# A two-layer graph network on one core: layer 1's turn with both halves of Y and their sums put first, and layer 0's gathers awaited by groups of 8 tiles

## The reference

```python
# layer 0: an edge network, summed over the edges of a destination
h = leaky_relu(concat(x[dst], x[src] - x[dst]) @ W1 + b1, 0.01)
h = leaky_relu(h @ W2 + b2, 0.01)
x = layernorm(x + segment_sum(h, dst))
# layer 1: attention with 4 heads, self loops added to the edges
xw = (x @ W).reshape(N, 4, 64)
logits = leaky_relu(a_src[src] + a_dst[dst], 0.2)
ex = exp(logits - segment_max(logits, dst)[dst])
alpha = ex / segment_sum(ex, dst)[dst]
x = layernorm(x + segment_sum(xw[src] * alpha, dst).mean(heads) + bias)
```

## Time and profile before

| | |
|---|---|
| median of three executions | 9346.02 us |
| profiled execution | 9348.76 us |
| its span (first to last instruction) | 9346.8 us |
| TensorE matmul busy | 6164.8 us, 66% |
| TensorE weight loads | 4718.3 us, 50% |
| VectorE | 5858.3 us, 63% |
| ScalarE | 3903.2 us, 42% |
| GpSimd | 6102.1 us, 65% |
| granted TensorE clock, mean | 0.863 |
| DMA | 301.41 MB, 32 GB/s |

### The profile page before, as it was taken

One profiled execution on the slowest core, in us unless ns is written; L12 is line 12 of the kernel. 1 busy time (PEld: TensorE's weight loads), 2 busy tenths in 40 slices (PEclk: granted clock), 3 DMA queues, 4 the chain that ended last, 5 costly groups with the idle time before them and its releaser, 6 DMA issues.

```text
span 9346.8 us, 206356 instructions
## 1 busy us (share of the span) xinstructions
PE 6164.8 (66%) x47166; PEld 4718.3 (50%) x47167; DVE 5858.3 (63%) x14312; ACT 3903.2 (42%) x10077; POOL 6102.1 (65%) x6281
## 2 busy tenths in 40 slices
PE   3477777777777767775366666666666666666675
PEld 2355555555555555553244444444444444444454
DVE  4355555555555555554477777777777777777753
ACT  1244444454444444442144444444444444444431
POOL 0777777777777777770577767676776767667600
PEclk6788888888888888996689989899998998989875
DMA  2211111111111111110311111111111111111100
GB/s 62 46 40 40 40 40 40 39 40 39 40 40 40 40 40 40 40 39 2 37 30 29 28 27 28 27 28 27 28 27 27 28 27 28 27 26 28 25 0 14
DMA packets 301370, 301.41 MB, mean 32 GB/s; under 512 B 194201, under 2 KB 197606, under 8 KB 301064
## 3 DMA queue, kind: packets, MB, share of 16 engines
q0 software_dynamic: 200704, 265.33, 15.2%
q1 hardware_dynamic: 98580, 32.69, 2.0%
q10 hardware_dynamic: 2068, 3.20, 0.1%
HBM read 286.10 MB, written 16.30 MB: 32 GB/s over the span
## 4 chain that ended last, share of the span: by engine, by line
DVE 23%; POOL 23%; issue 22%; PE 18%; DVEq 5%; ACT 3%; ACTq 2%; POOLq 1%; DMA 1%; SPq 0%
POOL big L361 23%; DVE S L464 7%; PE ps L905 6%; PE pu L891 4%; DVE state L655 2%; DVE rel L461 1%; DVE rowA L604 1%; POOLq L352 1%; DVE rowD L609 1%; PE ps L788 1%; DVE Y L636 1%; DVEq L671 1%; ACT ST L1063 1%; DVE zz L676 1%; DVE mnew L696 1%
## 5 line engine op out<-in xcount | busy, mean ns | idle before, releaser
L361 POOL DMA_INDIRECT big<-x_dram,idx x3136 | 3085.8, 984 | 1561.3 <-issue 1196.2
L361 POOL DMA_INDIRECT big<-q_dram,idx x3136 | 3015.3, 962 | 1201.8 <-issue 1197.3
L891 PE MATMUL pu<-Y,S 128*128 128x265 f32 x7856 | 2138.6, 417 | 746.2 <-DVE Y L636 738.9
L891 PEld LDWEIGHTS pu<-Y,S 128*128 128x128 f32 x7856 | 1489.9, 200 | 1035.2 <-issue 790.3
L636 DVE TENSOR_TENSOR Y<-big,ps 128x1040 f32<-128x1040 f32 x982 | 1210.1, 1232 | 659.8 <-ACT ps L1067 573.6
L464 DVE TENSOR_TENSOR S<-ps,rel 128x1024 f32 x978 | 1197.7, 1225 | 224.9 <-DVE rel L461 224.5
L981 ACT COPY ST<-ps 128x512 bf16<-128x512 bf16 x978 | 537.3, 586 | 1744.7 <-PE ps L788 1744.7
L802 PE MATMUL pu<-rowX,S 128*128 128x192 bf16 x3936 | 580.6, 264 | 1009.4 <-issue 765.7
L501 DVE TENSOR_TENSOR Y<-Y,rowX 128x512 f32<-128x512 f32 x491 | 340.5, 693 | 1256.9 <-ACT rowX L993 1238.9
L802 PEld LDWEIGHTS pu<-rowX,S 128*128 x3936 | 383.4, 98 | 1207.0 <-issue 1093.0
L905 PE MATMUL ps<-identb,S 128*128 128x128 bf16 x3912 | 550.6, 231 | 519.1 <-DVE S L464 518.5
(11 more groups left out here) (167 smaller groups left out, 8683.2 us busy)
## 6 DMA issues: line engine op xcount, KB each, us to landing
big<-q_dram,idx POOLq DMA_INDIRECT x3136
big<-x_dram,idx POOLq DMA_INDIRECT x3136
rowD<-dst_dram SPq DMA_DIRECT2D x196, 32.0 KB
q_dram<-state SPq DMA_DIRECT2D x3, 1568.0 KB, 20.2
x_dram<-big SPq DMA_DIRECT2D x1, 3381.0 KB, 39.8
idx<-srcT_dram SPq DMA_DIRECT2D x98, 32.0 KB, 1.8
dstc<-dstT_dram SPq DMA_DIRECT2D x98, 32.0 KB
out<-big SPq DMA_DIRECT2D x1, 3104.0 KB
```

Source lines behind the costliest of these rows:

```text
L361: nc.gpsimd.indirect_dma_start(o, None, x_dram if l else q_dram, bass.IndirectOffsetOnAxis(ap=idx[:, half, t:t + 1], axis=0)).then_inc(gat ...
L891: last = t_.matmul(bank, Sf[:, t, :], Y[:, t, :], start=(t == 0), stop=(t == 7))
```

## The change

In layer 1 the halves are no longer kept apart. VectorE does both `weigh` calls at the start of its turn, TensorE both `sums` calls before the transposes, and ScalarE exponentiates the weights `w` first in its turn and does both `ends` for turn n-1 (half 1 had been done a turn later). In layer 0 the gathers of a group raise a semaphore of their slot (16 of them, `slot`); SyncE waits for group after group, raises `ready`, and after eight groups `gdone`. TensorE waits for `ready` before each group and no longer for a chunk. SyncE's own work in layer 0 is written out: it counts a chunk's groups, then loads the lists of the chunk two further on. Core of the diff:

```diff
+        slot = [[sem(f"slot{p}{r}") for r in range(GS)] for p in range(2)]
+        ready = sem("ready")
...
-                 "lz": 1, "dw": 1, "w": 1, "sf0": 1, "sf1": 2, "y0": 2, "y1": 2, "U0": 2, "U1": 2, "nz": 3,
+                 "lz": 1, "dw": 1, "w": 1, "sf0": 1, "sf1": 1, "y0": 2, "y1": 2, "U0": 2, "U1": 2, "nz": 3,
...
+                if arrive is not None:
+                    arrive(g)
+                    apart(eng)
...
+            def landed(q, half):
+
+                apart(sp)
+                for r in range(GS):
+                    sp.wait_ge(slot[half][r], q * (16 * TG) + 16 * TG)
+                    sp.sem_inc(ready, 1)
+                sp.sem_inc(gdone, 1)
+
+            for i in range(2):
+                chunk(0, i, i)
+            with sp.Fori(0, (NS - 2) // 2) as q:
+                for half in range(2):
+                    landed(q, half)
+                    chunk(0, q * 2 + (half + 2), half)
...
-                            ).then_inc(gath[l][half], 16)
+                            ).then_inc(gath[half] if l else slot[half][r], 16)
...
                         weigh(k, 0, at)
+                        weigh(k, 1, at)
...
-                    if k.has(2):
-                        weigh(k, 1, at)
...
-                pe.wait_ge(gath[0][half], q * (16 * TS) + 16 * TS)
-                pe.sem_inc(gdone, 1)
-                steps(pe, 0, i, first0, turn0(half))
+                steps(pe, 0, i, first0, turn0(half), lambda g: pe.wait_ge(ready, g + 1))
...
                     sums(k, 0)
+                    sums(k, 1)
...
-                if k.has(2):
-                    sums(k, 1)
...
-                    if k.has(2):
-                        ends(k, 1, 2)
+                    if k.has(1):
+                        k.after("dw", 1)
+                        k.after("y1", 2)
+                        a_.activation(wb[:, :, :], dw[:, :, :], ACT.Exp).then_inc(m["w"], 1)
...
                     if k.has(1):
-                        ends(k, 0, 1)
+                        ends(k, 0)
...
                     if k.has(1):
-                        k.after("y1", 2)
-                        a_.activation(wb[:, :, :], dw[:, :, :], ACT.Exp).then_inc(m["w"], 1)
+                        ends(k, 1)
```

More of the change, by code:

```diff
@@ L157, in build @@
         dst_in = [sem("dst_in0"), sem("dst_in1")]
-        gath = [[sem(f"gath{l}{p}") for p in range(2)] for l in range(2)]
+        gath = [sem(f"gath{p}") for p in range(2)]
+        slot = [[sem(f"slot{p}{r}") for r in range(GS)] for p in range(2)]
+        ready = sem("ready")
         row_in = sem("row_in")
@@ L241, in apart, with steps @@
             eng.sem_inc(idle, 1)
-        def steps(eng, l, i, first, turn):
+        def steps(eng, l, i, first, turn, arrive=None):
             apart(eng)
@@ L294, in _, with chunk @@
             sp.wait_ge(s["t_out"], 32)
[L296 to L315, removed]
+            def chunk(l, i, half):
+                sp.wait_ge(gdone, i + (l * NS + 1))
+                sp.dma_start(idx[:, half, :], srcT_dram[:, ds(i * TS, TS)]).then_inc(idx_in[half], 16)
+                sp.wait_ge(fredge_flatd, i + (l * NS + 1))
+                sp.dma_start(dstc[:, half, :], dstT_dram[:, ds(i * TS, TS)]).then_inc(dst_in[half], 16)
@@ new lines, in landed @@
+            def landed(q, half):
[10 more added lines that the diff above has]
+                    chunk(0, q * 2 + (half + 2), half)
+            for i in range((NS - 2) // 2 * 2, NS):
+                landed(i // 2, i % 2)
+                if i + 2 < NS:
+                    chunk(0, i + 2, i % 2)
@@ new lines, in _, with chunk1 @@
+            sp.wait_ge(tab1["v"], 2 * (NB // 2) + 1)
+            sp.dma_start(x_dram.rearrange("(b p) d -> p b d", p=P), x1).then_inc(x_out, 16)
+            def chunk1(i, q, half):
+                chunk(1, i, half)
+                sp.wait_ge(sgv, i * 4 + 1)
+                for h in range(H):
+                    sp.dma_start(rowD[h * GS:(h + 1) * GS, :],
+                                 dst_dram[ds(i * (GS * GE), GS * GE)].rearrange("(g e) -> g e", g=GS)
+                                 ).then_inc(row_in, 16)
@@ L317, in _ @@
+            sp.wait_ge(s["d_out"], 32)
+            supers(sp, chunk1)
             sp.wait_ge(L[1]["acc"], STEPS + PAST)
@@ L592, in lk @@
                     dve.wait_ge(dvs, i * 8 + n)
-                dve.wait_ge(gath[1][half], q * (16 * TS) + 16 * TS)
+                dve.wait_ge(gath[half], q * (16 * TS) + 16 * TS)
                 dve.sem_inc(gdone, 1)
@@ L1027, in _, with ends @@
             copied(tab1, D)
-            act_tiles = Past(act, "act_tile", 2, 2 * TS - TG)
+            act_tiles = Past(act, "act_tile", 1, 2 * TS - TG)
             act_blocks = Past(act, "act_block", 3, NB - 1)
-            def ends(k, h, back):
-                k.after(f"U{h}", back + 1)
-                at = act_tiles.back(back - max(k.tail, 0))
+            def ends(k, h):
+                k.after(f"U{h}", 2)
+                at = act_tiles.back(1 - max(k.tail, 0))
                 a_.copy(Y[:, h * 4:h * 4 + 4, UW:YW], edgeE[:, ds(at + h * 4, 4), :])
-                a_.copy(Sf[:, h * 4:h * 4 + 4, :], S[:, ds(((k.sn + back) % 2) * TG + 4 * h, 4), :]
+                a_.copy(Sf[:, h * 4:h * 4 + 4, :], S[:, ds(((k.sn + 1) % 2) * TG + 4 * h, 4), :]
                         ).then_inc(L[1][f"sf{h}"], 1)
@@ L1052, in turn @@
                         a_.copy(Mx[:, ds(b, 1), :], mnew[:, :].unsqueeze(1)).then_inc(m["mb"], 1)
-                    if k.has(3):
                         k.after("e", 3)
```

## The result

The changed kernel takes **9692.75 us** (median of 3, 9691.95 to 9694.01) against 9346.02: ratio 1.0377, 95% interval 1.0363 to 1.0391. It is slower by 347 us, where the forecast was 8938 and the range ended at 9087. The profiled execution has a span of 9692.1 us.

What follows compares the result with a forecast made beforehand. GpSimd paces layer 0; turns of 7.63 us set layer 1's chunk, and GpSimd would after the change. Span 9346.8 less 400 (layer 0's 53 included) and 8 for the last chunk gives 8939; forecast 8938 us, range 8885 to 9087.

Steps and rivals of the forecast that it cites:

- Layer 0: End of layer 0: one turn of about 7 us behind the last landing instead of 60.5, so -53 us.
- The wait for `w`: Layer 1: VectorE's 1.31 us wait per turn for ScalarE's weights, before the first half of Y, goes.
- TensorE alone: Layer 1's turn, transposes to transposes: copy wait, `ad`, two sums; 6.5 us, and up to 0.4 for branch and waits.
- The 14.1 us of maxima and restart: Layer 1: the part of each chunk outside its turns, kept at 14.1 us beside 9.98 turns of 6.7.
- The clock: Rival: TensorE falls to 1.2 GHz in layer 1, turns up to 11.1 us; 9910 with half of them; chance 0.04.
- GpSimd's bound: Layer 1: unhindered gathers at 1.294 us each, 82.8 us a chunk, would set the pace after the change.
- the prediction's first rival: Layer 1's turn stays above 6.87 us and turns set the chunk: 9087 at 7.2 us, 8987 at 7.0; chance 0.25.
- The slower rival: TensorE at 1.2 GHz in layer 1; slower than before once a chunk passes 91.3 us; 9910 with half; chance 0.04.

Runs made afterwards that it cites:

- ad first: The changed kernel with `ad` moved from the end of TensorE's turn to the head of the next in layer 1: 8967.14 us, 8955.08 when repeated.
- the filled one: The kernel with `ad` at the head of the next turn, plus five unread matmuls behind each turn's transposes in layer 1: 8944.71 us, ratio 0.9569.
- fill_both: The changed kernel plus five unread matmuls behind the transposes and eight behind `ad`: first run 13506.34 us beside 13963.45 for the kernel before; repeat 9408.21 us.

## Why the prediction was wrong

- **Layer 0** was right in mechanism and low in size: -53 forecast, -65 to -70 measured alone. Groups are awaited (704.5 us of TensorE's idle time there end with SyncE's L313), one turn is left behind the last landing, and SyncE's counting held nothing up: the gathers of layer 0 wait for their own issue alone (1200.3 us). Why gathers run at 1.260 instead of 1.267 us in layer 0 wasn't tried.
- **The wait for `w`** went, as forecast: no idle time before Y ends with ScalarE in the kernel after. VectorE now waits for TensorE's sums there (550.6 us in the page's group of L660).
- **The step that failed** is the loop "TensorE alone": "6.5 us, and up to 0.4 for the turn's branch and waits, which no row shows apart here". The rows did show it. In the earlier trace rows the sums start at 7008.32, 1.25 us behind the `ad` before them, with VectorE's Y named as the releaser. But Y was done at 7007.59, 0.73 us before that start. What was left had no releaser but TensorE's own sequencer, and the rest of its work had run under half 1's matmuls, `ad` and the wait for Y. Bare, it is 1.76 us in 343 of the 441 turns and 0.51 in the other 98 (means over the gaps between the last `ad` and the first sums). Where it is 0.5, the turn is 6.65 us in the mean, as forecast. The forecast rested on the minority. A turn into a new group takes 7.70 us even where all of its sums run at full clock (125 of 343); by my estimate from these rows the mean turn would then be 7.47 us, hardly under the 7.67 of before. (The 14.1 us of maxima and restart grew as well, by 1.2 us a chunk: from a chunk's last S to the next one's first it is 22.4 us instead of 21.2.) So the exposed change of group alone takes away nearly all that the wait for `w` gave.
- **The clock** was a rival at 0.04, argued away by busy time, "5.1 of 6.7 us". But the change pushes TensorE's work into one block and its idle time into another, 3.4 us with only `ad` between, and it is behind this that the clock falls: of the 343 bursts of sums into a new group 125 run at full clock throughout, 131 start at it and fall to 1.2 GHz on the way, 87 start at 1.2 GHz; of those within a group, behind 0.5 us, only one has slow passes. The mean burst is 4.95 us instead of 3.8, and the mean of the 440 turns 8.45 us (from `ad` to `ad`) instead of the 7.47 at full clock: some 435 us, an estimate from the trace. The runs agree. With both idle times filled, the sums fell to 4.03 and the time by 285 us, net of some 75 us that the filling costs within groups. *The Trainium skill, TensorE: Matmul & The Clock Gate, section "HAM oscillation — how this bites in real kernels", bears on this: the trace agrees that waits between bursts cost the clock, by this pair of runs, but here only a quarter of the bursts (87 of 343) start at the half clock.* The two causes aren't independent, because the bare change of group is also what makes the idle time long; moving `ad` cures most of both, 726 us.
- **GpSimd's bound** of 82.8 us a chunk was right: with ad first its gathers take that. That this kernel and the filled one come within 30 us of the forecast 8938 is in part luck, though. Their turns are 7.03 and 6.98 us, not 6.7, and chunks of 83.7 and 83.4 us are still set by turns, which is the prediction's first rival (8987 at a turn of 7.0); the two limits just lie close together. What was forecast came close to true of a kernel one move away from this one.
- **The slower rival** would have given 9910 with half the turns at 1.2 GHz. Measured: 98.8 us a chunk, past its threshold of 91.3, with slow passes in about half the turns, but only some of each, and on top of a turn that was longer at full clock too.

## What to carry to other kernels

When the work of a loop's body is reordered, the sequencer's own work (branches, register loads, values read from memory) is an entry in each engine's loop, and it was hidden here only while instructions were already queued, or while the engine waited anyway. Where the turn is otherwise ready to be shorter, don't end a body on a short instruction that waits for another engine: put it at the head of the next, so that the loop's overhead runs in that wait. In the old order, where VectorE's wait for `w` set the turn, the same move gave nothing. And when a row names a releaser, compare its end with the start it is said to release: the handovers here take about 0.25 us, and the 0.73 us of the earlier trace rows was something else.

## What the runs showed of the hardware

- VectorE's multiplication of 128 x 1040 with both inputs in SBUF holds up GpSimd's indirect DMAs, with one input in PSUM hardly: gathers 1.126 against 0.988 us in the mean, one of 1.90 us beside it, 373 us in the kernel. *The Trainium skill, SBUF — State Buffer, section "Who interferes with whom", says that `tensor_tensor` with both inputs in SBUF contends with GpSimd's reads of SBUF, but infers that it doesn't stop descriptor generation; the measurement differs from the inference and decides, for an indirect DMA whose indices lie in SBUF. Whether the reads of the indices are what is held up, no run here shows.*
- A filled wait can make a kernel faster with more work: five added matmuls a turn took 154 us off the changed kernel.
- The same kernel can differ by half between rounds. In three of them the kernel before took 13.7 to 14.0 ms; the chip isn't what tells them apart, since chips 12 and 13 of the record stand in rounds of both kinds. In the profile of fill_both from there a gather is the usual 0.95 us, but 375 of layer 0's 3135 steps between gathers last over 3 us, every one at a change of group, and most of GpSimd's wait there ends with TensorE's turns (1772.6 us, L848). Why the turns are slower is open. Ratios from there aren't used.
